# A recurrence's sum over eight keys: first level added on VectorE, four identity products instead of eight, orders written anew

## The chip, the cores and the metric

One core of one Trainium2 chip runs the kernel. The metric is the device time of one execution in microseconds (us), as the median of several executions. The engines meant below are PE (TensorE, matrix products), DVE (VectorE), ACT (ScalarE), POOL (GpSimd) and SP (it issues the transfers). Each runs its own list of instructions in the order written; between engines only semaphores order the work.

## What is computed

Four layers on x of 16 sequences x 128 tokens x 256 channels: an RWKV layer, a cross attention on a context, another RWKV layer, another cross attention with an MLP. The change touches the recurrence of the RWKV layers (32 heads of 8 channels; s is an 8 x 8 state for each head):

```python
def step(s, inp):
    k_l, v_l, w_l, r_l = inp
    a = k_l[..., :, None] * v_l[..., None, :]
    out = jnp.einsum('bhs,bhst->bht', r_l, faaaa * a + s)
    s_new = a + w_l[..., None] * s
    return (s_new, out)
```

The output of a token is, for each of 8 value channels, a sum over 8 keys of r times the state. That sum over keys is what is divided otherwise. Everything is float32 but the biases and the masks.

## The kernel before, in words

The 16 sequences are worked in groups of four. Two RWKV layers and four groups make eight mixer units, R0 to R7 here; two attention layers and four groups make eight attention units, A0 to A7; the last ones are followed by four half MLP units. Three programs run beside each other on every engine. Program H (`head`) norms, mixes and projects the inputs of a mixer unit (decay, K, V, R, gate). Program R (`recurrence`) is the recurrence of a unit, its norm and its output projection, and in layer 1 the channel mix. Program A (`attn`) is an attention unit. `in_order` (L134) takes the three generators and a string of letters for each engine, `ORDER` (L104): each letter H, R or A lets that program issue its instructions up to its next `yield`. Such a piece is called a step below. The four strings are constants, so the order on an engine is fixed whatever the durations. Mixer units share their buffers (K_, V_, R_, W_, A_, S_ and half of PSUM, PA and PB), so the head of unit u+1 overlaps the recurrence of unit u only in part, and attention unit u overlaps mixer unit u+1.

A recurrence holds (head, batch) in 128 partitions. Its 8 value channels are taken as four chunks of two (`DC`, `NCH`). On DVE a unit goes: `outer` (L473) of chunks 0 and 1, that is K times V into A_[0] and A_[1]; the reduction that makes RU (L556), after POOL has multiplied R_, K_ and u (L780, L781); then for each chunk c two scans along time (L563, one for each value channel) into S_; and the product of R_ and S_ (L571), 2 x 8 x 128 elements in each partition, back into A_[c % 2]. After chunks 1 and 2 comes the outer product of the next chunk. On PE a chunk is the sum over the 8 keys: eight products of the identity with A_[c % 2][:, :, k], two channels x 128 tokens each (L1301), accumulated in PB. PE waits for that with `r_rs`, and `r_y` of a finished chunk lets its A_ buffer be written again: by `outer` (L473) and by ACT's `first_column` (L857). A float32 product stands as two records in the trace, so L1301 has 8 x 4 x 8 x 2 = 512. Before the last chunk comes an identity product of V_ (L1291), which POOL has scaled (L786).

Other steps that the text names: on PE the projections of K, V and R (L1267), whose last half for R must be done before POOL's product and so before RU; the low-rank mixes (L1184, L1198) with their DVE steps (L449, L458); the gate (L1281); and an attention's 16 jobs: scores (L1375, L1380) on PE, the maximum on DVE (L659), four exponentials on ACT (L1003), transposes on PE (L1393). The MLPs and the last attention unit follow the last recurrence, from about 964 us on.

Of the kernel before, what the change touches and what calls it, by code (L numbers as in the profile page):

```python
# [102 lines left out]

ORDER = {  # L104
    "VectorE":
        "HHHHHHHHHHHHAHHRRHHRRRRRRRRHRRRRHRHRRHHHRHHRRRRHRRHAAAAHHRRHAAHAAAARRRRAARHAAHRRAARRARARAHRAHAAAHRRR"
        "AAHHARRARRARAAHHHRRAAAAHHAAHHAAAHHARRAARRRRAARAARARRAARRAHAAHRARAARRHRHAAHARHHARRRHHHRAAAHARRAHAAAHA"
        "HAAAHHARRHHAARRRRHAAHAAHAHHRAARRAHAHAHRRRRRAAAHHRRRAAARHAHRRRARAARRRAHAAHARAAHHRRRRAAARARRAHAHRRRRAR"
        "AAHRARRHAHARHAHARRRARAAHAHARRRRRAAHHAARAAAAHHRRAARARRRAARRRARRAARARARRAHARHAARRAHHRAHAAHHRAARRRRHHAA"
        "RRRRAAHHARAHRHAARHHRRRRRAAARRAARARARAHHARARRAARAHAHARAAHARRRAAHHARARRARRAAHHAARARHHRRRRHHHRRAAAHRRAA"  # L110
        "RARARAARARARRAARRAARRARAARRRAAHHARRRRHARHAHARRARRARAAHHRRRHAAAAAAAAAAAAAAAAAAHHHAAAAAAAHHHAAAAH",
    "GpSimd":
        "HRRHAARRHAARRHAARHRARAHRRARRHRARAHRARARRHRAHAHHA",
    "ScalarE":
        "HHHHHHHHHHRHHRRRHRHRHRHHHHAHHAARAAHHAAAAAAAARAAAAAAAAHAAAAAAAARAAAHRAARARAHAARAAAAAAAHHHAHHAAAHHAHHR"
        "AAAAAAAAAAAARAAAAAAAAAAAAAARAHRARHARAAHARAHAAARAHAAHAHHAAAAHHHHAAAAHAAAAAAHAAAARAAAAHAAAHAAHAAAARRAH"
        "AHHARAARAHARAAHAAAAARHAHAAAHAAARAAAAARAAAAHRAHRAARAAHAHRAAAAAAAAHHAAHRARAAHAAHAAAAAAAARRRHHAAAAAARAA"
        "AAAAARAAAAAAHAAAAAAAHARRRAAHRAAHAHAAAAAHARHHAARRHHRAARAAHHAAAAAAAAAAAARAHAAAAAAAAAAAARAAAHAARRARAAAH"
        "RAAAAAAAHHHAAHHARRRAARHHAARAAHHAAAAAAAAAAARAAAAAAAAARAAARAARARAHRAAAAAAHAAHARHAARARAARAAAHAHHAAAAAAA"
        "AAAAAAAAAAAAAAAAHAHAHAAAAAAAAAAHAHAAAAAH",  # L120
    "TensorE":
        "HHHHHHHHHHHHHHHHHHHHHHHRRRRHHRRRRRRRRHRRRRRHHHHHRHRHHRHHAHHAHHAHHAAAHHAAAHHAAAAAHRHAAARARRAAHARRAAAA"
        "AHRRAAAAAARAARRRARAAAAHARRRRHHAAAAHARAAHARARAAHAHHHAHHAHAAHAAHHAHHHHAAAAAAARAAAAAARRHRAAARHAAAHRARHA"
        "ARAAAAAHAHARAAARRRRARRRRHAAHHAHHAARHAAHARAHHAARAHHHAHAAAAAHHAHHHHAHHHHAAHHAAAAAAAARAHRRARAAAAAHHAAAH"
        "HAARRHRHAAAARHAHRRRRARHAAAAHRRRRHHAAAAHAAARHRARAAAHHAHAHHHHHAAHAAAHRRRRAAAARAAARRRARARAARRAAAHRARRRH"
        "HARHHAAAAHAHRHAAHAAAAARARHHAAARHAAHRAHHAAAAAARAHAHAARRRAHHAAAAAARRRAAARHHRAAHHAAAARRRAARARAAAAHRHARA"
        "AAARRRARAHARAAAHHARHHRRHAAAHAAHAHARAHHAHAHRARHHRARHRHAAHAAHAAAAAAARRRHAAHHRAHAARARRAAAHHAAAAARAAAAAA"
        "AARARRHAAAAARRRRRRHAAAAHAARAHHRAAAAHAHRHAHAAHHARHHARRRHHRHAHRAAAAHAHAAAAAAAAARAAAARAARRRRAAAHARARAAA"
        "RRAHRAARHAAARHRRRRHAAAHAARRAARAHAHHAARHHARHAHAAARRARAARAAAHAHHAHHAAHAAAAAAAAAAAAAAAAAAAAHAAAAHAAHHAH"
        "HHAAAAAAHAAAAHHAHHHAAAAAAHAH",  # L130
}


# [1442 lines left out]
```

## Time and profile before

| what | value |
|---|---|
| median of 3 runs | 1146.26 us (1144.7 to 1146.98) |
| profiled execution: its time, its span | 1145.66 us, 1143.9 us |
| mean granted TensorE clock | 0.969 of full |
| PE busy | 1027.8 us (90%), 8866 records |
| PE weight loads busy | 772.4 us (68%) |
| DVE busy | 788.0 us (69%), 1078 records |
| ACT busy | 536.7 us (47%) |
| POOL busy | 108.4 us (9%) |
| chain that ended last | PE 61%, DVE 21%, ACT 9%, issue 4% |

The profile is one execution; times in it are counted from the start of the span. Busy is the union of an engine's records. Matrix products overlap in PE's pipeline, so the mean duration of one record is larger than the distance from one to the next. Shares over the whole span mix stages in which different engines are full, so most of the rows below are taken from stretches.

### The profile page before, as it was taken

The numbers are of one execution on the slowest core, as the hardware profiler recorded it, in microseconds if no ns is written. First come the engines' busy times: TensorE is split into PE (matmuls) and PEld (weight loads), VectorE is DVE, ScalarE is ACT, GpSimd is POOL, SyncE is SP. The second block draws the span as 40 slices with busy tenths as digits, with TensorE's granted clock in tenths as the row PEclk, the third lists the DMA queues.
The fourth block names the chain that finished last, engine by engine and source line by source line (L and its number), as shares of the span: only waits on it lengthen the run. The fifth ranks groups of instructions, "written<-read, shape, count | busy, mean of one in ns | idle before, by whom it ended". The sixth has DMA issues, their size and how long they took to land.

```text
span 1143.9 us, 21369 instructions
## 1 busy us (share of the span) xinstructions
PE 1027.8 (90%) x8866; PEld 772.4 (68%) x8866; DVE 788.0 (69%) x1078; ACT 536.7 (47%) x1643; POOL 108.4 (9%) x101
## 2 busy tenths in 40 slices
PE   7747899989998899988999799998999979999998
PEld 5634567766776667755777577786667757787777
DVE  3698579866996679789964998748965589623320
ACT  1102236742655255632576256634664346625662
POOL 1001010101010010021200201010100100100000
PEclk9978999999999899998999999999999989999999
DMA  9200010000000000000000000001000000000000
GB/s 375 83 0 1 2 30 11 1 2 22 20 1 2 15 22 6 2 2 19 19 5 1 27 14 2 1 2 44 6 1 2 29 22 1 1 1 22 26 10 19
DMA packets 17058, 24.80 MB, mean 22 GB/s; under 512 B 4417, under 2 KB 13761, under 8 KB 16322
## 3 DMA queue, kind: packets, MB, share of 16 engines
q1 hardware_dynamic: 16962, 23.44, 6.1%
q8 instruction: 70, 1.15, 0.4%
q14 instruction: 26, 0.21, 0.1%
HBM read 17.13 MB, written 2.10 MB: 17 GB/s over the span
## 4 chain that ended last, share of the span: by engine, by line
PE 61%; DVE 21%; ACT 9%; issue 4%; POOL 2%; DMA 2%; SPq 1%; DVEq 0%; ACTq 0%; POOLq 0%
PE PA L1267 7%; PE PB L1301 6%; PE QB L1380 5%; DVE S_ L563 5%; PE PB L1129 5%; ACT big L1003 4%; PE QA L1129 4%; PE QA L1393 3%; PE PA L1184 3%; PE QA L1119 2%; PE PA L1119 2%; DVE A L571 2%; PE QA L1404 2%; PE QA L1088 2%; PE QB L1088 2%
## 5 line engine op out<-in xcount | busy, mean ns | idle before, releaser
L1003 ACT ACTIVATE big<-QB,nmax 128x128 f32<-128x128 f32 x512 | 181.0, 374 | 95.6 <-DVE nmax L659 95.3
L563 DVE TENSOR_TENSOR_SCAN S_<-W_,A 128x1024 f32<-128x1024 f32 x64 | 146.0, 2303 | 1.9 <-ACT A L857 1.7
L1301 PE MATMUL PB<-A,common_w 128*128 128x256 f32 x512 | 128.5, 395 | 17.3 <-DVE A L571 17.2
L1380 PE MATMUL QB<-big,QX 128*128 128x256 f32 x512 | 134.8, 386 | 10.2 <-DMA QX<-big 10.2
L659 DVE TENSOR_REDUCE nmax<-QB 128x4 f32<-128x512 f32 x128 | 86.5, 685 | 57.8 <-PE QB L1380 56.4
L1301 PEld LDWEIGHTS PB<-A,common_w 128*128 128x128 f32 x512 | 98.0, 198 | 38.4 <-DVE A L571 20.9
L1380 PEld LDWEIGHTS QB<-big,QX 128*128 128x128 f32 x512 | 99.4, 195 | 28.9 <-DMA QX<-big 11.6
L1267 PE MATMUL PA<-X,rwkv_w 128*32 128x128 f32 x3072 | 97.6, 283 | 17.2 <-DVE X L458 16.9
L1003 ACT ACTIVATION_READ_ACCUMULATOR big<-QB,nmax 128x1 f32 x512 | 109.7, 214 | 0.0
L1267 PEld LDWEIGHTS PA<-X,rwkv_w 128*32 128x32 f32 x3072 | 85.8, 114 | 31.0 <-DVE X L458 23.8
L449 DVE SCALAR_TENSOR_TENSOR PA<-PA,rwkv_w,SX 128x512 f32<-128x512 f32 x80 | 56.4, 751 | 61.2 <-PE PA L1184 55.4
L1393 PE MATMUL QA<-common_w,big 128*128 128x128 f32 x512 | 78.4, 276 | 4.2 <-ACT CN L1012 3.1
L1393 PEld LDWEIGHTS QA<-common_w,big 128*128 128x128 f32 x512 | 60.9, 141 | 23.4 <-issue 9.9
L473 DVE TENSOR_TENSOR A<-K_,V_ 128x2032 f32<-128x2032 f32 x32 | 72.5, 2266 | 5.3 <-ACT V_ L892 4.2
L571 DVE TENSOR_TENSOR A<-R_,S_ 128x2048 f32<-128x2048 f32 x32 | 73.2, 2289 | 0.8
L1375 PE MATMUL QB<-mrow,first_row 128*128 128x512 bf16 x128 | 49.7, 388 | 16.7 <-ACT big L1003 14.0
L1184 PE MATMUL PA<-low,rwkv_w 32*128 32x256 f32 x256 | 45.4, 429 | 7.9 <-ACT low L868 2.2
L458 DVE TENSOR_TENSOR X<-PA,XN 128x512 f32<-128x512 f32 x80 | 51.3, 683 | 0.9
L1012 ACT ACTIVATE XT<-QA 128x512 f32<-128x512 f32 x64 | 38.6, 603 | 28.1 <-PE QA L1393 27.9
L958 ACT ACTIVATE big<-QB,attn_w,common_w 128x512 f32<-128x512 f32 x32 | 23.1, 773 | 55.8 <-PE QB L1088 55.8
L1012 ACT ACTIVATE CN<-QA 128x512 f32<-128x512 f32 x64 | 38.7, 604 | 19.5 <-PE QA L1393 19.4
L1129 PE MATMUL PB<-rwkv_w,S_ 128*128 128x256 f32 x192 | 46.1, 385 | 1.2 <-DVE S_ L598 1.2
(192 smaller groups left out, 1751.8 us busy)
## 6 DMA issues: line engine op xcount, KB each, us to landing
rwkv_w<-in_rwkv_w SPq DMA_DIRECT2D x2, 2866.0 KB, 14.5
QX<-big SPq DMA_DIRECT2D x128, 32.0 KB, 1.9
attn_w<-in_attn_w SPq DMA_DIRECT2D x2, 1031.5 KB, 16.8
mlp_w<-in_mlp_w SPq DMA_DIRECT2D x1, 2052.0 KB, 23.2
X<-in_x SPq DMA_DIRECT2D x4, 512.0 KB, 16.4
ctx<-in_ctx SPq DMA_DIRECT2D x4, 512.0 KB, 3.3
ctx<-in_ctx_t SPq DMA_DIRECT2D x4, 512.0 KB, 3.3
out<-XT SPq DMA_DIRECT2D x4, 256.0 KB, 2.0
```

The source lines that it names most:

```text
L473: return v.tensor_tensor(A_[c % 2][:, :, :, 1:T], K_[:, :, 0:T - 1].unsqueeze(1).broadcast_to([P, DC, RS, T - 1]), V_[:, DC * c:DC * c + D ...
L563: last = v.tensor_tensor_scan(S_[:, d].rearrange("p k t -> p (k t)"), W_[:].rearrange("p k t -> p (k t)"), A_[c % 2][:, d].rearrange("p k ...
L571: v.tensor_tensor(A_[c % 2][:], R_[:].unsqueeze(1).broadcast_to([P, DC, RS, T]), S_[:], ALU.mult)\
L659: v.tensor_reduce(nmax[:, n % 2], bank(2 + n % 2).rearrange("p (j s) -> p j s", j=JH), AX.X, ALU.max, negate=True).then_inc(sem["a_max"], 1)
L1003: last = s.activation(PR[:, n % 2, j], bank(2 + n % 2)[:, j * T:(j + 1) * T], ACT.Exp, bias=nmax[:, n % 2, j:j + 1], accum_out=den[:, b, h ...
L1012: s.activation(PT[n % QUAD], bank(0).rearrange("p (j t) -> p j t", j=JH), ACT.Copy)\
L1129: last = t.matmul(dst[:, (b - base) * C:(b - base + 1) * C], lhs(h, b), w[:, h], start=(h == 0 and b == 2 * k), stop=(h == HALF - 1 and bi ...
L1184: last = t.matmul(pa(h)[:, 256 * q:256 * q + 256], w2, low[rows:rows + MIX, 256 * q:256 * q + 256], start=True, stop=True, tile_position=( ...
L1267: last = t.matmul(PA[RH * b:RH * b + RH, k * T:(k + 1) * T], wt[:, h, RH * k:RH * k + RH], src[:, h, b * T:(b + 1) * T], start=(h == 0), s ...
L1301: last = t.matmul(y, ident, A_[c % 2][:, :, k], start=(c % 2 == 0 and k == 0), stop=False, skip_group_check=True)
L1380: last = t.matmul(o, QX[b % 2][:, i, h], K2[:, :, h, b * T:(b + 1) * T], start=False, stop=True, skip_group_check=True)
L1393: last = t.transpose(bank(0)[:, j * T:(j + 1) * T], PR[:, n % 2, j], ident)
```

## The change

On DVE, after the product of R_ and S_, a new step adds keys 4 to 7 onto keys 0 to 3 in place: `folded(c, 4)`, 2 x 4 x 128 = 1024 elements in each partition from two inputs. The product is now followed by a wait of DVE for itself (`link`) and the new step raises `r_rs`. On PE a chunk has four identity products instead of eight. DVE thus issues 32 instructions more (8 units x 4 chunks) and PE 256 records of products fewer, with 256 weight loads. The letters of all four engines are written anew: on VectorE 595 become 627 (32 for the new steps), on TensorE 828 become 764 (an R step held two products; a chunk had four such steps and has two), ScalarE and GpSimd keep their numbers of steps.

```diff
+FOLDED = 4
...
 ORDER = {
     "VectorE":
...
                 def recurrence(u):
                     xf = X2[u.lane][:].rearrange("p b c -> p (b c)")
+
+                    def folded(c, n):
+                        part = A_[c % 2]
+                        return v.tensor_tensor(part[:, :, 0:n], part[:, :, 0:n], part[:, :, n:2 * n], ALU.add)
+
                     yield
                     dve.wait_ge(sem["r_turned"], u.at("r_turned", 6))
                     link(outer(u, 0))
@@ -568,8 +574,9 @@
                         yield
                         if c == 0:
                             dve.wait_ge(sem["r_turned"], u.at("r_turned", 8))
-                        v.tensor_tensor(A_[c % 2][:], R_[:].unsqueeze(1).broadcast_to([P, DC, RS, T]), S_[:], ALU.mult)\
-                            .then_inc(sem["r_rs"], 1)
+                        link(v.tensor_tensor(A_[c % 2][:], R_[:].unsqueeze(1).broadcast_to([P, DC, RS, T]), S_[:], ALU.mult))
+                        yield
+                        folded(c, 4).then_inc(sem["r_rs"], 1)
                         dve.wait_ge(sem["r_rs"], u.at("r_rs", c + 1))
                         if 1 <= c < NCH - 1:
                             yield
@@ -1295,7 +1302,7 @@
                         yield
                         pe.wait_ge(sem["r_rs"], u.at("r_rs", c + 1))
                         y = PB[:, DC * c * T:DC * (c + 1) * T]
-                        for k in range(RS):
+                        for k in range(FOLDED):
                             if k and k % 2 == 0:
                                 yield
                             last = t.matmul(y, ident, A_[c % 2][:, :, k], start=(c % 2 == 0 and k == 0), stop=False,
```

How the letters lie around a recurrence, by counting them in the strings. Inside means: on VectorE from the RU step (L556) of the unit to the step that raises `r_rs` for chunk 3, without the unit's own steps.

| unit | H and A steps inside, before | after | steps that came in |
|---|---|---|---|
| R0 | 3 | 4 | one low-rank mix |
| R1 | 18 | 21 | a query bias, an update of x, a maximum |
| R2 | 16 | 17 | a query bias |
| R3 | 23 | 25 | two query biases |
| R4 | 13 | 17 | two low-rank mixes, a token shift, a mix |
| R5 | 16 | 22 | an update, norm statistics and two norms, a maximum, a normalisation |
| R6 | 23 | 23 | none |
| R7 | 13 | 18 | an output sum, statistics, a norm, a normalisation, a maximum |

No step left a stretch. In some chunks other steps stand between the product and its sum: for chunk 3 of R1 a norm of H, an update and a maximum. On TensorE three places count: from the identity products of a unit's chunk 3 to the next unit's last R projection; from there to chunk 0; from chunk 0 to chunk 3. In the first, for R1 to R4, the steps are nearly the same as before. For R5, seven steps leave it (the head's first products, which go ahead of chunk 3 of R4, and a job's transposes, the values of a sequence and an output projection of A3, which come after the R projection) and one comes in; for R6, six leave (a transposition and a job's transposes ahead, the four first MLP steps of A4 behind); for R7, five (an MLP projection of A5, keys, values and x transposes of A6), all to behind the R projection.

## Rows read from the trace of the kernel before

**Rows 1.** The page, part 1: busy us (share of the span) xinstructions.

```profile
PE 1027.8 (90%) x8866; PEld 772.4 (68%) x8866; DVE 788.0 (69%) x1078; ACT 536.7 (47%) x1643; POOL 108.4 (9%) x101
```

**Rows 2.** The page, part 4: shares of the chain that ended last, by line.

```profile
PE PA L1267 7%; PE PB L1301 6%; PE QB L1380 5%; DVE S_ L563 5%; PE PB L1129 5%; ACT big L1003 4%; PE QA L1129 4%; PE QA L1393 3%; PE PA L1184 3%; PE QA L1119 2%; PE PA L1119 2%; DVE A L571 2%; PE QA L1404 2%; PE QA L1088 2%; PE QB L1088 2%
```

**Rows 3.** Windows: start:end, length, busy (x) by engine, clock. RU to last product, R0 to R7.

```profile
59.48:100.07 40.59, 22.52 (x68) 15.36 (x68) 38.27 (x30) 2.86 (x6) 5.42 (x3) 0.76 0.00 0
166.23:214.88 48.65, 47.31 (x284) 35.88 (x282) 47.87 (x47) 30.29 (x115) 3.56 (x3) 1.00 0.06 13
284.18:333.40 49.22, 47.19 (x282) 35.20 (x281) 45.14 (x35) 29.70 (x113) 2.36 (x1) 1.00 0.06 13
409.41:468.40 58.99, 57.33 (x448) 42.18 (x446) 55.37 (x59) 33.08 (x120) 3.56 (x3) 1.00 0.05 11
515.24:567.04 51.80, 45.40 (x185) 32.62 (x183) 49.17 (x55) 20.00 (x57) 10.54 (x5) 0.93 0.07 20
648.21:695.98 47.77, 42.02 (x239) 30.29 (x239) 45.85 (x40) 20.59 (x87) 4.48 (x2) 0.93 0.07 16
770.24:831.84 61.60, 56.46 (x324) 40.71 (x323) 54.36 (x62) 32.14 (x117) 6.86 (x5) 1.00 0.08 23
917.22:963.43 46.21, 40.22 (x252) 31.09 (x252) 42.03 (x28) 23.70 (x103) 2.35 (x1) 0.93 0.06 14
sum 404.83, PE 358.44 PEld 263.34 DVE 378.05 ACT 192.35 POOL 39.14; mean PE 44.81 PEld 32.92 DVE 47.26 ACT 24.04 POOL 4.89
```

**Rows 4.** Windows of the parts between; the last is the tail, "sum" holds all eight.

```profile
100.12:159.10 58.98, 48.39 (x597) 34.63 (x598) 39.15 (x70) 17.29 (x28) 2.40 (x4) 0.91 0.01 1
...
833.10:912.10 79.00, 76.31 (x817) 58.46 (x815) 44.80 (x81) 40.09 (x97) 3.29 (x6) 1.00 0.03 11
963.80:1143.90 180.10, 168.46 (x975) 135.38 (x973) 58.77 (x124) 93.05 (x287) 8.51 (x16) 1.00 0.04 13
sum 625.58, PE 576.27 PEld 444.28 DVE 347.13 ACT 312.59 POOL 26.29; mean PE 72.03 PEld 55.53 DVE 43.39 ACT 39.07 POOL 3.29
```

**Rows 5.** Timeline of DVE, start, us, instruction: the last product (L571) of R1.

```profile
212.58 2.29 DVE L571 TENSOR_TENSOR A<-R_,S_ 128x2048 f32<-128x2048 f32 x1
```

**Rows 6.** Timeline of PE: the step before, and R1 chunk 3 (its first 14 records).

```profile
213.26 1.89 PE L1129 MATMUL QA<-attn_w,CT 128*128 128x256 f32 x8
214.99 3.22 PE L1301 MATMUL PB<-A,common_w 128*128 128x256 f32 x14
```

**Rows 7.** Timeline of PE: identity products of R0 chunk 0.

```profile
68.11 5.80 PE L1301 MATMUL PB<-A,common_w 128*128 128x256 f32 x16 [11.38 <-DVE A L571]
```

**Rows 8.** The chain that ended last, in order of time: start, us, what.

```profile
181.24 1.73 PE PB L1301 x8
100.12 3.72 PE PB L1301 x16
```

**Rows 9.** Line L1301: who waited for its products (us, times).

```profile
  ACT A L857: 8.4, 5
  DVE A L473: 0.8, 2
```

**Rows 10.** Lines: form, count, busy us, mean ns, idle before and releaser.

```profile
L563 DVE TENSOR_TENSOR_SCAN S_<-W_,A 128x1024 f32<-128x1024 f32 x64 | 146.0, 2303 | 1.9 <-ACT A L857 1.7
L1301 PE MATMUL PB<-A,common_w 128*128 128x256 f32 x512 | 128.5, 395 | 17.3 <-DVE A L571 17.2
L659 DVE TENSOR_REDUCE nmax<-QB 128x4 f32<-128x512 f32 x128 | 86.5, 685 | 57.8 <-PE QB L1380 56.4
L571 DVE TENSOR_TENSOR A<-R_,S_ 128x2048 f32<-128x2048 f32 x32 | 73.2, 2289 | 0.8
```

**Rows 11.** Lines of DVE: two-input instructions of 512 and of 1024 elements.

```profile
L439 DVE TENSOR_TENSOR SX<-XN 128x512 f32<-128x512 f32 x16 | 10.5, 689 | 8.1 <-ACT XN L826 8.1
L590 DVE TENSOR_TENSOR A<-PB,RU 128x1024 f32<-128x1024 f32 x8 | 9.8, 1224 | 0.2
```

**Rows 12.** Windows: clock while PE waits in R0 (fields as above).

```profile
60.00:69.00 9.00, 0.90 (x2) 0.81 (x3) 8.93 (x5) 0.00 (x0) 0.00 (x0) 0.50 0.00 0
```

More of the change, by code:

```diff
@@ L105 @@
     "VectorE":
[L106 to L110, printed above, removed]
@@ L111 @@
-        "RARARAARARARRAARRAARRARAARRRAAHHARRRRHARHAHARRARRARAAHHRRRHAAAAAAAAAAAAAAAAAAHHHAAAAAAAHHHAAAAH",
+        "HHHHHHHHAHHHHHHRRHRRRRRHRRRRRRRRRHRHRHRRRHHRHHHRRRRHHRRAAHHARARAAHHAAARARRRRAARHAHRRAARRHAARRAARRARA"
+        "HAARRRHAARHAARHRRRRAARHHHRAAAAHHAAAHHAAAHHRARARRARRRAARARARRAAHRARAHARRARRAAARRHRRHAAHRAHHARRHRHHARA"
+        "ARRAHHAAAAAHHAAAHHARRHHRARAHHRHRAHHRAARRHAAHRHARARRARRRAAARHHARARRRAAARHHARRRAARRAHAHRAARARAARRRRARH"
+        "HAARARRRAAHHRHAARRRRHARHARRRRHHAARRRRARHRHRRAAARAAARAAAHHARHHAARRRARARAARARRRAARHHAARRRARAARRHARRARA"
@@ L112 @@
+        "HARAHRAARRAHHRRRRRAHHARRARRAHAHARRHHAAAHAHRRRRRAARARRRAARHAHARARRARARRRARAHARAAHRAAAHRRRAAHHARAAHHAR"
+        "RRAARHHAARRRHHRRRRHHRRRAARARRAARRARARARARARAARRAARRARAAARRRAARAHHRARRRHARAHHARRRAARARRHHHRARAAAAAAAA"
+        "HAHHAAAAAAAAAAAAAAAHHHAAAAH",
     "GpSimd":
-        "HRRHAARRHAARRHAARHRARAHRRARRHRARAHRARARRHRAHAHHA",
+        "HRRHAARRHAARRHAARHRARAHRRRARHRARARHARRARHRAHAHHA",
     "ScalarE":
-        "HHHHHHHHHHRHHRRRHRHRHRHHHHAHHAARAAHHAAAAAAAARAAAAAAAAHAAAAAAAARAAAHRAARARAHAARAAAAAAAHHHAHHAAAHHAHHR"
@@ L116 @@
[L116 to L120, printed above, removed]
@@ L121 @@
-    "TensorE":
[L122 to L130, printed above, removed]
+        "HHHHHHHHHHHRRRHHRRHRHRHHHHAHHAAAHHAARAAAAAAAAAAHRAAAAAAAAAARAAAAAAHAARRARAAAHRAAAAAAAHHHAAHAHAHHHHRA"
@@ new lines @@
+        "AAAAAAAAAAAARAAAAAAAAAARAAAAAHRARAHRAAHARAAHAAAAHAAAHHHAAAHRHHAHHAAAAHAAAAHRAAAAAAAHAHAAAAAARAAAAAHR"
+        "RHHAAARAAHAAARHAAAAAHAHRAAAHRAAAAAAAHAAARHAARRAHRAHRHAAAAAAHAAAHAAAAARAAARHHAARARAAAHAAHARAAAAAARAAA"
+        "AAAHAAAAAAARAAAAAAARHARRAHRHAAHAAAAHARAAAHHRAAAHHRRRAAAHAHAAAAAAAAAARHAAAAAAAAARAAAAAAAAHARAARAHRAAA"
+        "AAAAHAAHARHHHARAHHARRRAAHHRAAAAAAAAAAAARAAAAAAAAAAARAAAARAARARAHAARAAAAHAAHAHAARARARRAHAAAAHHAAAAAAA"
+        "AAAAAAAAAAHAAAAAAHHAAAAAAAAAAAAHAHAAHAAA",
@@ new lines @@
+    "TensorE":
+        "HHHHHHHHHHHHHHHHHHHHHHHRHHRRRRHRRRRHHHHHRHRHHRHHHHAHHAAAAAHHHHAAAHAAAHHAHAAAAARHHARAAAARAARAAAAAAAAA"
+        "AARARAAAHRRRAAAHAAHRHARAHARAAAHAHHHHAHAAAHHAAHHAHHHHAAAHAAAHAAHRAARAAAHAAAAAAAAARRAAHAAAHRAAAAARARRR"
+        "HAAHHAHHARAHAARAHARAAHHAHAHHAHAAAAHHHHAHHAHHHHAHHAAAAHAAHAAAHARHHRAAAAAHRAAAAHRHAAARAHAAARRAHAAAARRH"
+        "HHAAAHAAAARHARHAHAARAHHAHHHAAAAAHRHHARAAAARAAAAARAHRAAHHAHHRRRRAAHHAAHRHARRAAAHAHAAAAAHRAAAHAAARAAHH"
+        "ARAAAHHRRRAHAHAAAAAAHAHAAHRHRAAAAAAHAHAARAARAAAAAAAAAAAARRHRRRAHAAAHARHHRRHHAHAHAAARAAHHARHAHRAHAHAH"
+        "RHRRAHHAAAAAAAAAAAHRHHHARAAAAAHAARRHAAAAAAAAAAAAAAARAAHRAAARRRHHAAHAHAAAAHAAHAARHHARHHRHAHAAARHHRHRA"
+        "HRRRAHHAAAAAAAARAAAAAARAAAAAAAARARAAAAAHHRAAAAHAAHRRRRAAHAHAARAARARAHHHAAHAHHARAHAARRRHARRAAAAAHAHAH"
+        "HAAHAAHAAAAAAAAAAAAAHAAAAAHAHAAAAAHHHAAAAAAAHAAAHAHAHHHAAAAAAAHH",
```

## The prediction

> **What bounds the kernel now.** Over the span PE looks like the bound: 90% busy, DVE 69% [rows 1], and the chain that ended last is mostly PE's, with L1301, the line that the change halves, at 6% and L571 at 2% [rows 2]. That average mixes two regimes, so I cut the span in two kinds of stretches. The first runs from the RU step of a recurrence to the end of its last product (L571), the stretch that "inside" means in the table of letters. There are eight, 404.8 us together, with DVE busy 378.05 (93%) and PE 358.4 (89%) [rows 3]. The other kind begins with the identity products of chunk 3 and ends with the next unit's last R projection, and the tail is its last: 625.6 us, PE busy 576.3 (92%), DVE 347.1 (55%) [rows 4]. What is left of 1143.9 us are 54 of start, ahead of R0's last R projection, 4 ahead of chunk 3 (below) and 55 between the second kind and the first (ACT's copy of the projection and POOL's two products; 159.10 to 166.23 us ahead of R1 [rows 3, 4]). In the second kind DVE has room and PE has hardly any; in the first kind DVE is the fuller one.
>
> Which of two full engines sets the end of a first stretch is seen at chunk 3: in R1 the product ends at 212.58 + 2.29 = 214.87 [rows 5], and PE takes up its identity products at 214.99 [rows 6]. It is the same at all eight: between the product's end and PE's start lie 0.0 to 2.0 us, 4.4 in sum. In the middle of a stretch PE runs up to 8 us behind DVE, but DVE doesn't wait for it: 0.8 us for L473 and 8.4 us of ACT's in all [rows 9]. So these stretches last as long as DVE's work in them, plus 26.8 us of DVE's idle time.
>
> **The change part by part.** *Identity products.* Eight records take 1.73 us at the full clock [rows 8], a chunk's 16 thus 3.46; 32 chunks give back 55.4 us of PE, some more where the clock is low (3.72 and 5.80 us for 16 in R0 [rows 7, 8]). Of this, three chunks in four lie within the first kind of stretch, 41.5 us, where PE isn't what ends them. I cost that gain at nothing; the cover is DVE's work, and should DVE be the lighter one there, it is worth up to the 41.5. The fourth chunk comes at the head of the second kind, where PE has the next work at hand: 8 x 1.73 = 13.8 us, gained.
>
> *The added sum.* No row shows two SBUF operands of 1024 elements. Bounds: 0.69 us for 512 [rows 11] and 2.29 for 2048 [rows 10]; the line through both gives 0.69 + 512 x (2.29 - 0.69)/1536 = 1.22, and 1024 elements with one operand in PSUM take 1.22 too [rows 11]. 32 x 1.21 (they start somewhat closer than their length) = 38.7 us, all of it inside the first stretches, on the engine that ends them. The new wait of DVE for its own product holds up what stands behind it, but it is of the kind that already stands between the scans and the product, which DVE reached with 0.8 us of idle time in 32 times [rows 10]: 0 to 1 us. POOL's and SP's queues aren't passed.
>
> *The new orders inside.* 22 steps of H and A come into the first stretches and none leaves. Priced by the distances between starts in this trace (maximum 0.6, query bias 0.7, low-rank halves 1.4 and 1.25, norms of four sequences 1.7 to 2.5, shift and mix 2.7) they are 1.3, 2.1, 0.7, 1.4, 5.3, 8.0, 0 and 6.4 us for R0 to R7: 25.2. With the sums, DVE's work inside becomes 378 + 38.7 + 25.2 = 442 us.
>
> *Idle time inside.* DVE waited 26.8 us there, partly for scores (L659 [rows 10]) that PE was late with. PE now has 41.5 us less to do inside, so that part should go. I take 13 of the 26.8 as left; bounds 3 and 32. First stretches: 442 + 13 = 455 against 404.8, so +50 (+40 to +69).
>
> *What the orders move out of the second kind.* For R1 to R4 and the tail PE's steps there stay nearly as they are. For R5 to R7 they lose attention and MLP work that now stands behind the last R projection: priced in the same way 4.6, 8.2 and 11.4 us, 24 together (eight records of 256 columns 1.73 us [rows 8]). There it fills the 14 to 20 us that PE has between that projection and chunk 0; for R6 it is some 5 us too much, which the middle chunks, where PE now has room, take up. With the identity products the second kind loses 13.8 + 24 = 38 us of PE work. All of it counts only if the 49 us of PE's idle time there [rows 4] stay as they are; around R1 to R3, where PE idled 9.6 of 59 us for R1 [rows 4] and the head's chain of DVE and ACT steps sets the pace, the gain can shrink. Bounds: 20 and 42; I take 38. The lags at chunk 3 fall from 4.4 to about 2: -2 (-4 to +2).
>
> *Sum.* +50 - 38 - 2 = +10 us. The profiled execution took 1145.66 us (its span 1143.9); that stands 0.6 below the median of 1146.26, so 1156. By the bounds the forecast's own range is 1146.26 + 40 - 42 - 4 = 1140 to 1146.26 + 69 - 20 + 2 = 1197; with not all ends at once, 1144 to 1180.
>
> **A rule weighed against this.** The rows give PE as the busiest engine, 90% to 69%. The Trainium skill, Perfetto Trace Analysis, section Identifying the Most-Contended Engine, says to optimise the engine with the highest occupancy first; by it the whole 55 us count. The same page, section Optimization Strategy, says that a kernel can have several regimes with another engine contended in each. The stretches above agree with the second sentence; the first is the fourth rival.
>
> **The rivals.**
>
> *1, faster: PE holds the inside too.* In R1, R2 and R3 PE is busy 97, 96 and 97% inside [rows 3], and the chain that ended last goes through PE there. Then halving L1301 takes half of its 6% of 1143.9 us, -34; the sums lengthen the chain only where products lie on it: L571 has 2%, 23 us, 10 products of 32, so 10 x 1.21 = +12. That gives 1146 - 22 = 1124. For it: that chain, which in R1 runs through L1301 [rows 8], and orders that may close part of the 49 us of PE's idle time outside. Against it: DVE's 98% inside R1 and 93% over all, and chunk 3, where PE never came late by more than 2 us. It decides if DVE's work inside stays below the stretch's length less what PE saved, which the 442 us deny.
>
> *2, even.* DVE's idle time inside falls to about 4 us and the outside gains its full 42: +41 - 42 = -1; with the lags 1144 to 1148.5.
>
> *3, clearly slower: a sum that waits behind others.* Where other steps stand between a product and its sum (2.9 us in R1's chunk 3), and with PE less full inside, PE stands still for longer ahead of each chunk. In R0 it did so for 8 us and was granted 0.50, that is 1.2 GHz, from 60 to 69 us [rows 12]; the 16 records after it took 5.80 us for 3.46 [rows 7, 8], 2.3 lost. If this happens once in each of the eight units at the head of a second stretch (+18) and DVE's idle time inside stays at 26.8 (+14 on the forecast), while the outside gain holds, the time is 1156 + 32 less the part that falls together, about 1180. It decides once the wait ahead of chunk 3 grows from below 1 us to several.
>
> *4: the whole gain of PE.* 1146 - 55 = 1091, with the sums all hidden. DVE has 356 us of idle time in the span [rows 1], but only 26.8 of it inside, where the sums stand.
>
> **How the numbers follow.** Forecast (1148.6 to 1170) 0.44; clearly slower (1170 to 1195) 0.15; even 0.12; faster by PE's chain (1110 to 1144) 0.26; whole gain 0.03. A measurement of this kernel can tell about 0.2%, 2.3 us, from no change. So slower by more than that 0.59, same 0.12, faster 0.29. The range leaves out the fourth rival, the lower part of the first (together about 0.1) and the end of the third (0.08): 1126 to 1182.
>
> **What would show it.** In the profile after: L1301 with 256 records and about 64 us busy; a new DVE line of 32 two-input instructions of about 1.22 us; DVE 825 to 828 us busy and PE about 965. The eight stretches from RU to the last sum: 445 to 470 us in all, DVE over 95% busy and PE near 80%; the other kind near 588. PE's waits for the sum at L1301 grow well above the 17.2 us that L571 cost [rows 10]. The forecast is wrong if these stretches stay near 410 us (the first rival), or if the second kind shrinks by much more than 38 us because the idle time in it goes too.

## The result and the profile after

The changed kernel takes 1161.84 us in the median (1161.03 to 1168.36, 5 runs) against 1146.26 (5 runs): a ratio of 1.0147, 95% interval 1.0133 to 1.0160, so 15.6 us slower. The profiled execution is the one that took 1168.36 us, with a span of 1166.4 and a mean granted clock of 0.947; the other four took 1161.0 to 1162.5 us at 0.950 or 0.951, so some 6.5 us of the profile below are that execution's own.

The page of after, parts 1 and 4, which answer [rows 1, 2]:

```profile
PE 995.6 (85%) x8610; PEld 733.8 (63%) x8610; DVE 823.0 (71%) x1110; ACT 535.9 (46%) x1643; POOL 110.5 (9%) x101
```

```profile
PE 52%; DVE 30%; ACT 8%; issue 4%; POOL 3%; DMA 2%; SPq 1%; DVEq 0%; ACTq 0%; POOLq 0%
DVE S_ L569 8%; PE PA L1274 7%; PE PB L1136 5%; PE QB L1387 4%; DVE A L577 4%; PE QA L1136 4%; ACT big L1010 4%; PE PA L1191 3%; DVE A L474 3%; DVE nmax L666 3%; PE QA L1126 2%; PE QA L1400 2%; PE PA L1116 2%; DVE A L553 2%; PE PA L1126 2%
```

PE is busy 32 us less, DVE 35 us more, and in the chain that ended last PE fell from 61 to 52% and DVE rose from 21 to 30%. The product of R_ and S_ (L577 now) and the new sum (L553) are on it.

Windows of after from the RU step to the end of the last sum, R0 to R7, with the columns of [rows 3]:

```profile
59.89:105.86 45.97, 17.81 (x43) 10.95 (x44) 44.36 (x35) 3.29 (x7) 5.42 (x3) 0.61 0.00 0
173.20:229.02 55.82, 45.04 (x270) 32.06 (x269) 54.83 (x54) 30.01 (x116) 3.55 (x3) 1.00 0.05 11
299.52:351.47 51.95, 44.22 (x262) 31.07 (x260) 50.91 (x39) 29.28 (x113) 2.35 (x1) 1.00 0.05 12
427.64:490.80 63.16, 54.82 (x427) 38.16 (x426) 61.05 (x65) 33.57 (x121) 5.45 (x3) 1.00 0.05 11
534.86:599.77 64.91, 49.95 (x203) 32.51 (x201) 60.42 (x67) 22.67 (x62) 9.06 (x5) 0.91 0.06 16
668.10:729.70 61.60, 47.66 (x265) 31.44 (x263) 57.52 (x65) 29.04 (x107) 6.64 (x5) 0.97 0.07 19
798.68:864.56 65.88, 56.45 (x303) 39.67 (x302) 58.08 (x66) 31.82 (x117) 8.52 (x5) 0.92 0.08 22
937.11:991.47 54.36, 44.80 (x266) 31.46 (x264) 50.21 (x42) 28.57 (x112) 3.56 (x3) 0.97 0.08 21
sum 463.65, PE 360.75 PEld 247.33 DVE 437.41 ACT 208.24 POOL 44.55; mean PE 45.09 PEld 30.92 DVE 54.68 ACT 26.03 POOL 5.57
```

404.8 became 463.7 us. DVE's busy time went from 378.05 to 437.41, so its idle time inside stayed at 26, while PE's share fell from 89 to 78%. The other kind of stretch, as in [rows 4]:

```profile
106.38:168.09 61.71, 52.59 (x590) 37.40 (x589) 38.66 (x70) 17.42 (x26) 2.40 (x4) 0.81 0.01 1
229.33:294.43 65.10, 56.99 (x709) 43.01 (x708) 42.72 (x78) 28.30 (x72) 2.40 (x4) 0.92 0.01 3
351.51:421.69 70.18, 58.26 (x716) 43.32 (x717) 47.26 (x93) 30.59 (x79) 3.61 (x6) 0.93 0.03 9
...
865.94:929.58 63.64, 62.42 (x756) 48.24 (x754) 39.02 (x66) 33.42 (x85) 2.09 (x4) 1.00 0.01 2
991.53:1200.00 208.47, 166.40 (x966) 133.70 (x965) 57.71 (x122) 93.19 (x288) 8.06 (x16) 1.00 0.03 11
sum 619.18, PE 543.12 PEld 418.75 DVE 325.76 ACT 297.11 POOL 22.89; mean PE 67.89 PEld 52.34 DVE 40.72 ACT 37.14 POOL 2.86
```

The last window reaches beyond the span's end at 1166.4, so it is 174.9 us long and the sum 585.6, against 625.6 before. PE is busy 33 us less in them. R1's (the first row) is 61.7 us long against 59.0, at a granted clock of 0.81 against 0.91.

The instructions of the sum (L553) and of the identity products (L1308), each with who waited and for whom:

```profile
L553 DVE TENSOR_TENSOR A<-A x32: 1161/1224/1226, 68.5 to 990.3; 128x1024 f32<-128x1024 f32 x32
...
  PE PB L1308: 29.6, 8
```

```profile
L1308 PE MATMUL PB<-A,common_w x256: 379/379/797, 69.8 to 993.1; 128*128 128x256 f32 x128
...
  DVE A L553: 65.0, 21
```

The sum lasts 1.22 us. The 65.0 us add up two rows of the same waits: weight loads stood for it 13 times, 35.4 us in all, and in 8 of these the products behind them too, 29.6 us. So PE waited 35.4 us for the sum; before, it waited 20.9 us for the product (17.2 at the products themselves [rows 10]). 21.8 of the 29.6 us lie in R0; outside R0 the products wait 7.8 us for 0.6 before. The place of the third rival, R1's chunk 3, on DVE's timeline (start, us, instruction) and on PE's:

```profile
222.84 2.29 DVE L577 TENSOR_TENSOR A<-R_,S_ 128x2048 f32<-128x2048 f32 x1
225.17 0.17 DVE L514 COPY XN<-st 128x8 f32<-128x8 f32 x1
225.25 1.38 DVE L422 TENSOR_SCALAR X<-X,mv,rstd 128x256 f32<-128x256 f32 x4
226.54 0.75 DVE L695 SCALAR_TENSOR_TENSOR X<-QA,tanh_gate,X 128x512 f32<-128x512 f32 x1
227.20 0.68 DVE L666 TENSOR_REDUCE nmax<-QB 128x4 f32<-128x512 f32 x1
227.80 1.22 DVE L553 TENSOR_TENSOR A<-A 128x1024 f32<-128x1024 f32 x1
```

```profile
226.68 1.09 PE L1086 MATMUL PA<-common_w,X 128*128 128x128 f32 x8 [2.89 <-DVE X L422]
227.61 1.88 PE L1298 MATMUL PB<-V_,common_w 128*128 128x512 f32 x4
229.33 1.89 PE L1308 MATMUL PB<-A,common_w 128*128 128x256 f32 x8
```

The product ends at 225.13, the sum begins 2.7 us later behind a norm of H, an update and a maximum. PE uses the time for H's transposition and the product of V_, and takes chunk 3 up 0.3 us after the sum: between sum and PE's start lie 2.6 us over all eight units.

### The profile page after: what moved, and what is told of

Same layout as the page of the kernel before. It is cut to its first block, busy times and chain, and to the rows that moved or that the text cites. A ratio compares the mean times of both kernels' runs of the same rounds, so it can differ in the third digit from the quotient of the medians.

```text
span 1166.4 us, 20898 instructions
## 1 busy us (share of the span) xinstructions
PE 995.6 (85%) x8610; PEld 733.8 (63%) x8610; DVE 823.0 (71%) x1110; ACT 535.9 (46%) x1643; POOL 110.5 (9%) x101
## 4 chain that ended last, share of the span: by engine, by line
PE 52%; DVE 30%; ACT 8%; issue 4%; POOL 3%; DMA 2%; SPq 1%; DVEq 0%; ACTq 0%; POOLq 0%
DVE S_ L569 8%; PE PA L1274 7%; PE PB L1136 5%; PE QB L1387 4%; DVE A L577 4%; PE QA L1136 4%; ACT big L1010 4%; PE PA L1191 3%; DVE A L474 3%; DVE nmax L666 3%; PE QA L1126 2%; PE QA L1400 2%; PE PA L1116 2%; DVE A L553 2%; PE PA L1126 2%
## 5 line engine op out<-in xcount | busy, mean ns | idle before, releaser
L1387 PE MATMUL QB<-big,QX 128*128 128x256 f32 x512 | 137.3, 392 | 9.9 <-DMA QX<-big 9.9
L1387 PEld LDWEIGHTS QB<-big,QX 128*128 128x128 f32 x512 | 100.9, 198 | 27.8 <-DMA QX<-big 12.0
L1274 PE MATMUL PA<-X,rwkv_w 128*32 128x128 f32 x3072 | 102.8, 293 | 11.5 <-DVE X L459 11.4
L1274 PEld LDWEIGHTS PA<-X,rwkv_w 128*32 128x32 f32 x3072 | 90.6, 118 | 23.4 <-DVE X L459 16.5
L1308 PE MATMUL PB<-A,common_w 128*128 128x256 f32 x256 | 70.5, 408 | 29.7 <-DVE A L553 29.6
L1308 PEld LDWEIGHTS PB<-A,common_w 128*128 128x128 f32 x256 | 48.7, 201 | 44.6 <-DVE A L553 35.4
L577 DVE TENSOR_TENSOR A<-R_,S_ 128x2048 f32<-128x2048 f32 x32 | 73.2, 2289 | 0.8
L1382 PEld LDWEIGHTS QB<-mrow,first_row 128*128 128x128 bf16 x128 | 12.6, 99 | 64.8 <-ACT big L1010 57.9
L1019 ACT ACTIVATE XT<-QA 128x512 f32<-128x512 f32 x64 | 38.7, 605 | 22.8 <-PE QA L1400 22.4
L1136 PE MATMUL QA<-attn_w,CT 128*128 128x256 f32 x192 | 45.6, 383 | 2.5 <-DVE CT L685 1.5
L793 POOL TENSOR_TENSOR V_<-V_,RU 128x1024 f32<-128x1024 f32 x8 | 19.3, 2416 | 295.5 <-DVE A L474 295.5
## 6 DMA issues: line engine op xcount, KB each, us to landing
attn_w<-in_attn_w SPq DMA_DIRECT2D x2, 1031.5 KB, 17.5
X<-in_x SPq DMA_DIRECT2D x4, 512.0 KB, 17.2
```

The lines of the kernel that those rows point to most:

```text
L577: link(v.tensor_tensor(A_[c % 2][:], R_[:].unsqueeze(1).broadcast_to([P, DC, RS, T]), S_[:], ALU.mult))
L1136: last = t.matmul(dst[:, (b - base) * C:(b - base + 1) * C], lhs(h, b), w[:, h], start=(h == 0 and b == 2 * k), stop=(h == HALF - 1 and bi ...
L1274: last = t.matmul(PA[RH * b:RH * b + RH, k * T:(k + 1) * T], wt[:, h, RH * k:RH * k + RH], src[:, h, b * T:(b + 1) * T], start=(h == 0), s ...
L1382: t.matmul(bank(2 + n % 2), first_row[:], mask, start=True, stop=False, skip_group_check=True)
L1387: last = t.matmul(o, QX[b % 2][:, i, h], K2[:, :, h, b * T:(b + 1) * T], start=False, stop=True, skip_group_check=True)
```

## The experiments

What they measured is gathered here once. Stretches come from each kernel's profiled execution: *inside* as in [rows 3]; *outside* as in [rows 4], but to PE's last record (622.4 for 625.6 before); *to RU*, from the last R projection to RU; *lag*, from the end of the last product or sum to PE's chunk 3. The clock is the mean granted one of that execution. "Old" and "new" are the orders of before and after. Ratios are against runs of before on the same chip (medians 1146.1 to 1146.7).

| kernel | orders, products, sum | median us | profiled us | clock | inside | DVE busy in it | outside | to RU | lag |
|---|---|---|---|---|---|---|---|---|---|
| before | old, 8, no | 1146.3 | 1145.7 | 0.969 | 404.7 | 378.0 | 622.4 | 55.3 | 4.5 |
| e2 | old, 4, no | 1138.6 | 1145.2 | 0.953 | 400.7 | 376.9 | 626.9 | 54.7 | 2.9 |
| e12 | as e2, filled | 1133.5 | 1134.3 | 0.974 | 400.8 | 377.0 | 617.5 | 55.0 | 2.3 |
| e3 | old, 8, yes | 1180.2 | 1180.4 | 0.962 | 439.4 | 417.0 | 625.1 | 54.7 | 0.7 |
| e1 | old, 4, yes | 1181.5 | 1177.2 | 0.948 | 439.4 | 415.8 | 620.8 | 54.7 | 3.1 |
| e5 | new, 8, no | 1171.3 | 1172.9 | 0.959 | 445.9 | 394.3 | 583.2 | 60.3 | 22.8 |
| e4 | new, 4, no | 1140.2 | 1140.2 | 0.958 | 432.7 | 394.6 | 572.9 | 60.1 | 15.1 |
| after | new, 4, yes | 1161.8 | 1168.4 | 0.947 | 463.7 | 437.4 | 582.3 | 59.9 | 2.6 |
| e6 | as after, filled | 1161.6 | 1161.8 | 0.965 | 464.3 | 437.1 | 575.8 | 60.4 | 2.2 |
| e9 | old, POOL's sum | 1185.9 | 1185.6 | 0.940 | 437.3 | 395.6 | 627.1 | 54.7 | 7.5 |

**The change without its orders (e1).** The sum directly behind its product, as part of the same step, and two of a chunk's four PE steps empty; then the old letters fit.

```diff
+                        part = A_[c % 2]
+                        v.tensor_tensor(part[:, :, 0:4], part[:, :, 0:4], part[:, :, 4:8], ALU.add).then_inc(sem["r_rs"], 1)
...
+                            if k >= 4:
+                                continue
```

> The whole change without the new orders: the sum stands right behind its product in the old VectorE order, and the two later steps of a chunk on TensorE are empty. Theory D (DVE's work sets the end of the eight stretches from RU to chunk 3): +39 for the sums inside, -14 for the identity products of chunk 3, that is 1146 + 25 = 1171 us (1163 to 1177), so the new orders gave back some 10 us. Theory P (PE's chain sets them): 1146 - 34 + 12 = 1124 us.

Measured: 1181.52 us (1177.17 to 1182.69), ratio 1.0293 (1.0267 to 1.0319). The row that sums its inside windows:

```profile
sum 439.50, PE 336.61 PEld 234.26 DVE 415.83 ACT 194.17 POOL 40.45; mean PE 42.08 PEld 29.28 DVE 51.98 ACT 24.27 POOL 5.06
```

The stretches grew by 34.7 us with 3 us less idle time of DVE: the sums' 39.2 us (32 x 1.224) went through nearly whole, as the forecast's mechanism says. But nothing came back: outside only 1.6 us went, where the forecast's 13.8 of chunk 3 should have. The orders of after are worth 20 us to the whole change. How much of the loss is the lower clock (0.942 to 0.948, against 0.957 to 0.962 in e3 below) is open: e1 was not run with the filling that follows.

**Each half by itself, in the old orders (e2, e3).** In e2 only the four products are left (`if k >= 4: continue` on before), in e3 only the sum is added.

> Old orders, no sum on VectorE, but only four identity products in a chunk (keys 4 to 7 are left out). It is PE's saving alone. Theory D: only chunk 3's products count, 1146 - 14 = 1132 us (1124 to 1138). Theory P: the halved line takes 34 us off the chain, 1112 us; all 55 us would give 1091.

> Old orders, eight identity products as before, and the sum on VectorE right behind its product (keys 4 to 7 are counted twice). It is DVE's cost alone. Theory D: all 32 sums show, 1146 + 39 = 1185 us (1178 to 1190). Theory P: only those on the chain, +12, 1158 us.

Measured: e2 1138.63 us (1133.28 to 1145.15, 9 runs), ratio 0.9931 (0.9906 to 0.9957). e3 1180.18 us (1176.55 to 1182.81), ratio 1.0285 (1.0253 to 1.0317).

```profile
sum 439.40, PE 367.64 PEld 265.75 DVE 417.03 ACT 195.13 POOL 40.38; mean PE 45.95 PEld 33.22 DVE 52.13 ACT 24.39 POOL 5.05
```

e3 settles that DVE ends the inside: 39 us of sums cost 33.5. e2 gives back 8 us of 55, so the first and the fourth rival are gone as far as the inside is concerned: it stayed at 400.7. But the executions of e2 differ by 12 us, and with them the granted clock: 1133.3 and 1133.5 us at 0.968, 1138.6 at 0.961 and 0.962, 1141.4 and 1144.4 at 0.955, 1145.2 at 0.953. The profiled one is the slowest.

**The same with the clock kept up (e12, e6, e7, e10, e11).** Where PE stands ahead of chunks 0 and 2 of R0 and at the head of H's unit 1, it multiplies 128 columns into PSUM that nobody reads; nothing else changes. e12 is e2 with that (44, 29 and 27 such products), e6 is after with it (46, 32, 32), e7 is before with it (44, 20, 15).

```diff
+                        if u.index == 0:
+                            keep_clock(QB[:, 0:P], {0: 44, 2: 29}.get(c, 0))
```

> Old orders, four identity products and no sum (keys 4 to 7 left out), with filling products while PE waits in R0 (44, 29, 27). Without filling it took 1139 us, from 1133 at a clock of 0.968 to 1145 at 0.953. Theory C: at the clock of the kernel before the products of chunk 3 give the 14 us that were forecast, 1132 us (1129 to 1135). If filling in R0 does nothing, or the clock falls elsewhere: 1139 us.

Measured: 1133.47 us (1132.79 to 1134.28), ratio 0.9889 (0.9874 to 0.9904), at 0.974 to 0.977. The clock row of the page's part 2 (tenths of full speed in 40 slices), for e2, then for e12:

```profile
PEclk9966799988999999998999989999999999999999
```

```profile
PEclk9988999999999999988999999999999999999999
```

and the stretch ahead of R1, again e2's and then e12's, which lost 5.5 us with it:

```profile
101.10:163.90 62.80, 51.59 (x589) 35.77 (x587) 38.97 (x70) 17.28 (x28) 2.41 (x4) 0.84 0.01 1
```

```profile
99.70:157.00 57.30, 46.59 (x590) 32.61 (x591) 39.01 (x70) 16.30 (x26) 2.40 (x4) 0.91 0.00 1
```

So halving the products, alone and with the clock kept, is worth 12.6 us against before and 11.5 against before with filling (e7 below), near the 13.8 that I had for chunk 3. The place isn't the one I gave, though: by the table's rows outside fell by 4.9, inside by 3.9 (R0's to R2's units, R4's and R5's), the lags by 2.2. In R6's and R7's part and the tail nothing came, although PE was busy 1.3 to 1.5 us less in each: e2's row for R7's,

```profile
832.80:912.00 79.20, 74.90 (x809) 56.90 (x808) 45.57 (x82) 39.95 (x97) 3.29 (x6) 1.00 0.04 11
```

answers the second of [rows 4]: PE busy 1.4 us less, the length 79.2 for 79.0. PE's timeline of e2 shows where the time freed went: right behind chunk 3 it waits 1.09 us for a mixed tile from DVE (L432), and at 841.16 it waits 0.83 us for a tile from ACT (L1012), where it waited 0.32 before.

> The changed kernel with products of the identity into unused PSUM while PE waits in R0 anyway (46 ahead of chunk 0, 32 ahead of chunk 2, 32 ahead of the head of unit 1), so that the clock isn't lowered. Theory C (part of what halving the products should have given back is lost to a lower TensorE clock, 124 us at half rate in the changed kernel against 73 before, two thirds of them in the first 150 us): the part between R0 and R1 goes from 61.7 to about 55, 1155 us (1152 to 1158). If the clock there is covered by DVE's work: 1162 us, no change.

> The kernel before with the same kind of filling products (44 ahead of chunk 0, 20 ahead of chunk 2, 15 ahead of the head of unit 1). Theory C: 27 us of its 73 at half rate lie in 58 to 117 us, most of them beside DVE's work; the head of unit 1 gains 2 to 4 us: 1143 us (1141 to 1145). If the clock is covered: 1146 us.

Measured: e6 1161.56 us (1159.51 to 1164.3), ratio 1.0135 (1.0116 to 1.0154), at 0.963 to 0.968. e7 1144.93 us (1142.42 to 1150.27, 10 runs), ratio 0.9990 (0.9976 to 1.0004), at 0.970 to 0.981; that can't be told from before. So in after the lower clock is no cause of the loss: at 0.965 as at 0.951 the median is the same. e6's profiled execution is like after's ordinary ones and serves below as the one to compare; of the profile's extra 6.5 us its R1 part (56.3 for 61.7 us) has 5.4.

**The new orders by themselves (e4, e5).** e4 is after without the sum, its step left empty; e5 has the eight products too, four in each of a chunk's two PE steps.

> The changed kernel, its orders and its four identity products, with the sum on VectorE left out (keys 4 to 7 are not added); its step is empty and the product releases PE. Theory D: the stretches become shorter by the 32 sums of 1.22 us: 1162 - 39 = 1123 us (1116 to 1130). Theory P: 1162 - 12 = 1150 us.

> The new orders with the old work: eight identity products in a chunk (two steps of four instead of four of two), no sum on VectorE. Theory D with PE as the second bound: DVE's work inside is 38.7 us less than in the changed kernel, but PE gets its 41.5 us inside back; the variant without sum and with four products took 1140 us with PE already 15 us late at chunk 3, so most of the products show: 1155 us (1148 to 1170). If orders and products were independent of each other (eight products cost the 8 us that they cost in the old orders): 1148 us.

Measured: e4 1140.19 us (1137.54 to 1144.05), ratio 0.9942 (0.9923 to 0.9962). e5 1171.28 us (1169.32 to 1175.03), ratio 1.0222 (1.0198 to 1.0246). The inside rows of e4 and e5:

```profile
sum 432.80, PE 347.13 PEld 239.49 DVE 394.63 ACT 204.34 POOL 44.54; mean PE 43.39 PEld 29.94 DVE 49.33 ACT 25.54 POOL 5.57
```

```profile
sum 446.10, PE 376.86 PEld 271.76 DVE 394.34 ACT 202.53 POOL 44.51; mean PE 47.11 PEld 33.97 DVE 49.29 ACT 25.32 POOL 5.56
```

At the identity products themselves PE waited 17.5 us for DVE in e5, three times, and 16.7 of them in R0; in e4 20.4 us, 18.3 of them in R0. Elsewhere it nearly always came late.

Neither expectation holds, and this pair shows most. With the new orders, halving the products is worth 31 us, four times as much as with the old ones: e5 has 445.9 us inside with DVE busy 394, so DVE idles 52 us there, and PE comes to chunk 3 late by 22.8 us in sum, in each of the eight units (0.4 to 4.8 us). Of the 52 us, DVE waited 25 for the scores (L1387), where it waited 12 inside before. PE has become the engine that ends these stretches in good part. And the sums cost 21.7 us instead of 33.5: from e4 to e6, inside grows by 31.6, but the lag falls by 12.9, since PE was late for chunk 3 anyway.

**The sum directly behind its product, in the new orders (e8, e11).** Nine of the 32 sums stand elsewhere in after; e8 moves these letters of VectorE forward, e11 is e8 with the filling (46, 32, 32).

```diff
-...HHARRHHRARAHHRHRAHHRAARRHAAHRHARARRARRRAAARHH...
+...HHARRHHRARAHHRHRRAHHRAARRHAAHRRHAARRARRRAAARHH...
```

> The changed kernel with each sum directly behind its product: in nine of 32 chunks one to three other steps stand between them, and go behind the sum here. Theory D: DVE's work is the same, and only what stood ahead of the sum of chunk 3 (2.9 us in R1, 1.3 us in R7) leaves the stretch: 1162 - 3 = 1159 us (1156 to 1162). Rival 3 (PE stands still too long ahead of each chunk because of these steps): 1150 us or less.

> The variant with each sum directly behind its product (1174 us, where 1159 was expected), with filling products of the identity while PE waits in R0 (46, 32, 32). Its profiled execution took 1167 us at a mean clock of 0.949, the others 1172 to 1177 at 0.940 to 0.946. Theory C (what the variant lost over the changed kernel was a lower clock in most executions): 1160 us (1157 to 1164), equal to the changed kernel with filling. If the sums' new places themselves cost the 12 us: 1174 us as without filling.

Measured: e8 1174.4 us (1166.72 to 1177.28), ratio 1.0254 (1.0226 to 1.0281), at 0.940 to 0.949. e11 1170.03 us (1165.51 to 1174.34), ratio 1.0208 (1.0184 to 1.0232), at 0.955 to 0.966. Both theories missed e8: the sums that stand later cost nothing where they are, moving them forward costs 8 to 13 us. DVE's and PE's timelines of e8 in R1's chunk 3:

```profile
217.94 2.29 DVE L577 TENSOR_TENSOR A<-R_,S_ 128x2048 f32<-128x2048 f32 x1
220.26 1.23 DVE L553 TENSOR_TENSOR A<-A 128x1024 f32<-128x1024 f32 x1
221.52 0.17 DVE L514 COPY XN<-st 128x8 f32<-128x8 f32 x1
221.60 1.38 DVE L422 TENSOR_SCALAR X<-X,mv,rstd 128x256 f32<-128x256 f32 x4
```

```profile
223.03 1.32 PE L1086 MATMUL PA<-common_w,X 128*128 128x128 f32 x8 [4.15 <-DVE X L422]
224.16 3.38 PE L1298 MATMUL PB<-V_,common_w 128*128 128x512 f32 x4
227.37 1.89 PE L1308 MATMUL PB<-A,common_w 128*128 128x256 f32 x8
```

Now H's norm stands behind the sum, and PE's transposition of its result stands ahead of chunk 3 on PE, so PE waits 4.15 us for the norm where after has 2.89, L1298 takes 3.38 us in place of 1.88 (the granted clock is 0.5 there, 223.8 to 227.2 us, and 1.0 in after at this place), and PE begins chunk 3 at 227.37: 7.1 us behind the product's end, against 4.2 in after. These 2.9 us are a part of what the profiled execution shows, and it is e8's fastest: its span is 5.0 us longer than e6's. From RU to chunk 3 it takes 4.9 us more in R1 and another 4.7 in R3, R6 and R7, and some 5 come back in other stretches. Of the median's loss, e11 shows that a part follows the clock (1165.5 us at 0.966, 1174.3 at 0.955) and that 8 us in the median do not go away with the filling. Where they lie stays open.

**The sum on POOL (e9, e10).** POOL makes the sum of chunks 0 to 2, PE has four products there and eight for chunk 3; old orders, POOL's letters longer by 24. e10 is e9 with the filling (50, 28, 15).

```diff
+                    for c in range(3):
+                        yield
+                        pool.wait_ge(sem["r_rs"], u.at("r_rs", c + 1))
+                        part = A_[c % 2]
+                        q.tensor_tensor(part[:, :, 0:4], part[:, :, 0:4], part[:, :, 4:8], ALU.add).then_inc(sem["r_pf"], 1)
```

> The old orders of VectorE, ScalarE and TensorE; the sum of keys 4 to 7 onto 0 to 3 is made by POOL, for chunks 0 to 2 alone, and these have four identity products; chunk 3 has eight and no sum. VectorE has nothing to add. POOL is 9% busy and takes 2.4 us for 1024 elements of two operands (L780, L786 before), 24 times. Theory D: the stretches inside keep their 405 us, since PE has time between chunks; of PE's gain some shows as in the variant with four products and no sum (1139 us): 1142 us (1137 to 1147). If chunk 0 to 2 reach PE too late, or POOL slows VectorE down: 1152 us or more.

> The same with filling products of the identity into unused PSUM while PE waits in R0 (50 ahead of chunk 0, 28 ahead of chunk 2, 15 ahead of the head of unit 1), which keep the clock up there. In the variant with four products and no sum, executions at a mean clock of 0.968 took 1133 us and at 0.953 1145 us. Theory C: the same dependence here, so 3 to 5 us under the variant without filling: 1138 us (1134 to 1143). If filling does nothing, as in the changed kernel: equal to the variant without.

Measured: e9 1185.89 us (1182.14 to 1187.58), ratio 1.0338 (1.0323 to 1.0354). e10 1179.08 us (1173.31 to 1185.83), ratio 1.0275 (1.0238 to 1.0312). POOL's sum by line, and the page's part 5 of e9 (line, engine, operation, tiles, count | busy us, mean ns | idle before):

```profile
L787 POOL TENSOR_TENSOR A<-A 128x1024 f32<-128x1024 f32 x24 | 68.8, 2866 | 244.1 <-DVE A L571 244.1
```

```profile
L563 DVE TENSOR_TENSOR_SCAN S_<-W_,A 128x1024 f32<-128x1024 f32 x64 | 154.0, 2427 | 2.3 <-ACT A L862 2.1
L1311 PE MATMUL PB<-A,common_w 128*128 128x256 f32 x320 | 94.7, 443 | 67.7 <-POOL A L787 63.5
...
L473 DVE TENSOR_TENSOR A<-K_,V_ 128x2032 f32<-128x2032 f32 x32 | 79.9, 2498 | 4.6 <-ACT V_ L897 4.2
```

The whole loss is larger than that of the sum on DVE. A sum on POOL lasts 2.87 us in the mean, PE waited 63.5 us for them, and DVE, which adds nothing here, was slowed: its scans last 2427 ns in the mean against 2303 [rows 10], its outer products 2498 against 2266 in the trace of before. The timelines show that this is a queue and not a general slowing. In R2, POOL's and DVE's rows, first with POOL's sum ahead, then with DVE's outer product ahead:

```profile
335.43 2.35 POOL L787 TENSOR_TENSOR A<-A 128x1024 f32<-128x1024 f32 x1 [14.25 <-DVE A L571]
```

```profile
336.00 3.92 DVE L473 TENSOR_TENSOR A<-K_,V_ 128x2032 f32<-128x2032 f32 x1
```

```profile
316.70 2.27 DVE L473 TENSOR_TENSOR A<-K_,V_ 128x2032 f32<-128x2032 f32 x1
```

```profile
316.75 4.43 POOL L787 TENSOR_TENSOR A<-A 128x1024 f32<-128x1024 f32 x1 [11.30 <-DVE A L571]
```

The one that comes second lasts until the first has ended and then about its own usual length (2.27 us on DVE, 2.34 on POOL). This happens to six of the 24 sums (4.38 to 4.43 us; the other 18 took 2.34 to 2.37) and to nine scans and six outer products, up to 4.36 us, which together last 17.1 us longer than 2.275 each; before, two scans were held up, by 1.7 us. A maximum (L659), which reads PSUM, lasts its usual 0.69 us beside the sum. Inside, DVE is busy 395.6 us instead of 378.0 without an instruction of its own more, nearly all of it these held-up ones, and idles 15 us more; over the span its waits for scores grew from 56.4 us [rows 10] to 70.8, PE being late with them. The executions of e10 fall in two groups, 1173.3 to 1173.7 us at 0.965 and 1184.4 to 1185.8 at 0.952 to 0.955.

The Trainium skill, Perfetto Trace Analysis, section Optimizing Scalar/DVE Operations, says that GPSIMD and DVE share a read port of SBUF, so that offloading between the two might not help. The rows of e9 agree: DVE's scans and outer products, with two operands in SBUF, and POOL's sums waited for each other.

## Why the prediction was right, and where it wasn't

The forecast was 1156 us (1126 to 1182, slower with 0.59); measured were 1161.84. The sign and the mechanism hold: the sums go through DVE, which ends the inside stretches, and most of PE's 55 us isn't on the path. The table's change from before to e6, whose profiled span (1159.8) is that of after's ordinary executions, is: inside +59.6, outside -46.6, to RU +5.1, lag -2.3, start and end 0; together 16. That the total came within 6 us is in part luck: inside was 9.6 us more than forecast and to RU 5.1 more, and outside gave 8.6 more back. Term by term:

*The sum's price.* 1.224 us against 1.21 to 1.22, 32 times: right. Its effect without the orders, +33.5 (e3), right too. The wait for the product just ahead cost nothing that shows: the profile has no idle time of DVE before the 32 sums.

*DVE's work inside.* 437.4 us against 442. The steps that came in are 20 us instead of 25; a part of that is that for R7 the list of letters ahead of the prediction is one place off (from A4's second update on, statistics were taken for the update next to them): what came in there are a norm, two query biases, an update and a maximum, some 4.7 us and not 6.4.

*DVE's idle time inside* is the step that failed: 13 us forecast, 26.2 measured, as much as before. I had argued that PE, with 41.5 us less to do, would no longer be late with the scores; inside, DVE waited 11.8 us for them before and 11.0 in after. The new orders use that room at once: e5's 52 us of idle time show what these orders cost on PE without the halving, e4's 38 and after's 26 what halving and sums leave of it. The gain of PE went into orders that need it, not into DVE's waiting. This +13, which the bounds held (up to 32), is more than the whole miss.

*Outside.* -38 forecast, -40 in the profile, -46.6 with the clock up (e6). The sum was nearly right and both its terms were off. The orders alone moved 39 us (e5, 583.2 for 622.4) and not 24: R5 7.6, R6 9.6 and R7 14.0 against 4.6, 8.2 and 11.4, and 8 more in R4, R1 to R3 and the tail that I had taken as unchanged. The products of chunk 3 gave 7.4 (e5 to e6, with the sums) or 10.3 (e5 to e4, without them) and not 13.8: 1.2 to 1.7 us in each of R4's to R7's parts and the tail, where 1.73 was the price, and in R1's to R3's together 0.6 us lost (e6) or 2.8 gained (e4), which the bound of 20 had in view. Of R1's part I had PE's idle time wrong by one: [rows 4] give 59.0 less 48.4, 10.6 us and not 9.6. In the old orders the same products gave 4.9 (e12), and 1.6 or nothing where the clock fell (e1, e2).

*The way to RU.* I had it at 0, and it took 5 us more: R4 9.6 to 13.6, R6 5.2 to 11.3, R7 5.1 to 7.5, while R1's, R3's and R5's got 6.6 us shorter together. What the orders move behind the R projection isn't PE work alone. After R6's projection, ACT's timeline of after shows the copies of R_ (L899) behind MLP activations (L1055) that wait for their products (L1116). These are moved steps: PE began them at 787.35, behind the projection.

```profile
789.38 0.84 ACT L1055 ACTIVATE big<-QA,mlp_w 128x256 f32<-128x256 f32 x2 [3.45 <-PE QA L1116]
...
791.84 0.60 ACT L899 ACTIVATE R_<-PA 128x512 f32<-128x512 f32 x1
792.84 0.84 ACT L1055 ACTIVATE big<-QB,mlp_w 128x256 f32<-128x256 f32 x2 [0.40 <-PE QB L1116]
793.57 0.60 ACT L899 ACTIVATE R_<-PA 128x512 f32<-128x512 f32 x1
```

The projection ended at 787.4; POOL's product waited for the copies to 794.2 and RU began at 798.7. I had priced the moved steps on PE and passed over ACT's queue, in which the copies stand behind what waits for these steps.

*The rivals.* The first (PE ends the inside) is false for the kernel before, by e2 and e3, and in good part true for the new orders without the halving, by e5: which engine ends a stretch depends on the orders. The fourth went with it: e2 would have been near 1091, and it took 1138.6. The Trainium skill, Perfetto Trace Analysis, section Identifying the Most-Contended Engine, has the engine of the highest occupancy go first, but it judges TensorE by MFU (its arithmetic as a share of the peak) and by the busy share of its weight loads, not by that of its products. I had taken the 90% of the products. The weight loads were busy 68% and DVE 69% [rows 1], so the section doesn't put PE ahead here, and the runs, in which DVE decides inside, don't speak against it. Of the third, the waits for the sum (35.4 us for 20.9) and the clock are there: the mean granted clock of 0.947 is, with the two levels of 1.2 and 2.4 GHz, 124 us at half rate (0.106 of 1166.4), against 71 us before. But it doesn't decide: e6 has 81 us and the same median. And its condition, a sum behind other steps, isn't what cost time in sum: e8, which takes it away, was slower.

*The signs.* The inside stretches (463.7 us for 445 to 470), the other kind (585.6 for 588), DVE's busy time (823 us for 825 to 828) and the sum's 1.22 us came as named, DVE's share inside nearly so (94% for over 95). PE's busy time didn't: 995.6 us for about 965. L1308 lost 58.0 us (128.5 to 70.5), but the rest of PE's work was busy 26 us longer, with 53 us more at half rate; what else it may be was not taken apart.

No kernel that computes the whole recurrence was faster than before; e7 comes closest and can't be told from it.
